# Attention with GpSimd exponentials: wider blocks every third round, the weighing two rounds behind the scores, roots as powers, another first stage and end

## The chip, the core and the metric

The kernel runs on one core of a Trainium2 chip. Its engines have a queue each and meet through semaphores: TensorE (PE in the rows; PEld is its weight load), VectorE (DVE), ScalarE (ACT), GpSimd (POOL) and SyncE (SP), whose queue issues most DMAs. The metric is the device time of one execution, in microseconds; the median of several counts.

## What is computed

One transformer layer with adaptive norms on 4096 tokens of width 256, 16 heads of 16 elements, hidden width 1024.

```python
h = _layernorm(x, axis=-1) * (1 + ca) + sa
x = x + ga * _L0_attn_ref(h, L0_attn_Wq, L0_attn_Wp, L0_attn_bp)
h = _layernorm(x, axis=-1) * (1 + cb) + sb
x = x + gb * _L0_ffn_ref(h, ...)

def _L0_attn_ref(x, Wq, Wp, bp):
    q = jnp.einsum('bnhd,hed->bnhe', xh, Wq)
    scores = jnp.einsum('bnhe,bmhe->bhnm', q, q)
    attn = jax.nn.softmax(scores / NORM, axis=-1)
    res = jnp.einsum('bhnm,bmhe->bnhe', attn, q)
    return res.reshape(B, N, D) @ Wp.T + bp
```

`_L0_ffn_ref` is a norm, two quantised matrix products with a silu between them, and half of the result added to its input. The heavy part is the softmax: 16 x 4096 x 4096 exponentials.

## The kernel before

**First stage** (the first `nc.Block`). The tokens go by in 8 tile groups of 512. For each group VectorE takes the statistics (`stats_of`), the root (`rsqrt`, a bit trick and three Newton steps: 12 small instructions, each waiting for the one ahead), and the normalised tokens (`normalise`, into `z_tok`, two slots). TensorE transposes them (`turn`, L477) and multiplies by `wq_diag`, feature side (L499) and token side (L511). ScalarE rounds to half precision (L440), VectorE keeps the rest (`split`, L582), and SP stores both to DRAM, from where `keys` and `asks` are loaded. VectorE's queue is in an order written by hand: statistics of groups 0 and 1, a root for both, then later groups between the splits.

**Main stage** (the second block). There are 8 x 4 = 32 *groups*: 512 asking tokens (index `c`) times 4 heads. A group has 64 *pairs* of score tiles (a pair is two 128 x 512 tiles, of one head). Three pairs make a *round*, 683 in all; `FIRST[gg]` is the round with which group `gg` begins. In a round:

- TensorE writes the scores of three pairs into six PSUM banks (L894).
- ScalarE takes the exponential of the first two pairs straight from PSUM (L857, 2048 columns).
- VectorE copies the third pair to SBUF (`copy_scores`), which frees its banks early, and ScalarE takes the exponential there (L863, 1024 columns).
- In the rounds of `SPARE_ROUNDS` (292 of the 683) the last `SPARE` = 128 columns of the third pair are GpSimd's: VectorE scales and clamps them (L1092), and GpSimd works out the exponential in eleven instructions of 128 columns (L825 to L841, here called a block); ScalarE then has 896 columns. `has_spare` gives every second round to GpSimd, but none from the 7th to the 20th round of the first group of an asking tile.
- `weigh` multiplies the exponentials with the values (L908), in *units* of four heads, one or two in a round. It waits for `exps_done` and, where a pair has GpSimd columns, for `spare_done`.

TensorE and VectorE run ahead: in the loop turn of round `at` both first serve the scores of round `at + BEHIND` (`scores_of`, `copy_scores`), and then do the weighing and everything else of `at`. `BEHIND` is 1, and `probs` has `P_RING` = 15 places for pairs.

Between these lie the projection, the norms and the feed-forward part of the asking tile before, cut into 40 pieces of TensorE work for each tile (`PIECE_IN`). Their norms are VectorE's, in the first group of the next tile: `norms(o, r)` in round `FIRST + r`. At r = 12 the second half of `x1` is there, and the moments follow (`bn_aggr`, L1121); at 13 and 14 the root; at 15 and 16 the scaling (`modulate`); at 17 and 18 statistics and moments again; at 18 and 19 the second root; at 20 the second norm. GpSimd has nothing to do with these.

**End.** The last asking tile has no attention beside it: sums, projection, norms and feed-forward run in a row, in two `PARTS` of two tiles each.

Of the kernel before, what the change touches and what calls it, by code (L numbers as in the profile page):

```python
# [10 lines left out]
P = 128  # L11
BANK = 512
# [25 lines left out]
S_RING, P_RING, K_RING = 3, 15, 4  # L38
BEHIND = 1
# [3 lines left out]
RSQRT_STEPS = 12  # L43
# [10 lines left out]
PARTS = [(0, 2), (2, 4)]  # L54

# [45 lines left out]
SPARE = 128  # L101
# [8 lines left out]
def has_spare(at):  # L110

    gg = max(g for g in range(GROUPS) if FIRST[g] <= max(at - BEHIND, 0))
    c, group = divmod(gg, Q_GROUPS)
    r = at - BEHIND - FIRST[gg]
    return at % 2 == 0 and at + 1 < ROUNDS and not (c > 0 and group == 0 and 7 <= r <= 20)


SPARE_ROUNDS = [at for at in range(ROUNDS) if has_spare(at)]
# [39 lines left out]


def rsqrt_guess(dve, y, v, work, step, n):  # L160

    shifted, v_eps = work[:, 0, :], work[:, 2, :]
    k = n * RSQRT_STEPS
    dve.tensor_scalar(v_eps, v, EPS, None, ALU.add).then_inc(step, 1)
    dve.wait_ge(step, k + 1)
    dve.tensor_scalar(shifted.bitcast(I32), v_eps.bitcast(I32), 1, None, ALU.logical_shift_right).then_inc(step, 1)
    dve.wait_ge(step, k + 2)
    dve.tensor_scalar(y.bitcast(I32), shifted.bitcast(I32), -1.0, float(0x5F3759DF), ALU.mult, ALU.add).then_inc(step, 1)


def rsqrt_steps(dve, y, work, step, n, steps):

    square, v_eps = work[:, 1, :], work[:, 2, :]
    k = n * RSQRT_STEPS
    for i in steps:
        dve.wait_ge(step, k + (3 + 3 * i))
        dve.tensor_tensor(square, y, y, ALU.mult).then_inc(step, 1)
        dve.wait_ge(step, k + (4 + 3 * i))
        dve.scalar_tensor_tensor(out=square, in0=square, scalar=-0.5, in1=v_eps, op0=ALU.mult, op1=ALU.mult).then_inc(step, 1)
        dve.wait_ge(step, k + (5 + 3 * i))  # L180
        dve.scalar_tensor_tensor(out=y, in0=square, scalar=1.5, in1=y, op0=ALU.add, op1=ALU.mult).then_inc(step, 1)


def rsqrt(dve, y, v, work, step, n):

    rsqrt_guess(dve, y, v, work, step, n)
    rsqrt_steps(dve, y, work, step, n, range(3))
    dve.wait_ge(step, (n + 1) * RSQRT_STEPS)


def adaln_layer(nc, x, wq_t, wp_t, bp, gamma, beta, fc1_q, fc1_s, fc1_b, fc2_q, fc2_s, fc2_b,
# [9 lines left out]
    with ctx:  # L201
# [56 lines left out]
        rsqrt_work = a.take("rsqrt_work", 3 * 5 * GT).rearrange("p (s t) -> p s t", s=3)  # L258
# [26 lines left out]
        stats_done, moments_done, rstd_done, z_ready = sem("stats_done"), sem("moments_done"), sem("rstd_done"), sem("z_ready")  # L285
# [73 lines left out]
        with nc.Block() as block:  # L359

            @block.sync
            def _(sp):
# [41 lines left out]

                sp.wait_ge(shift_split, 1)
                first_shifts(sp, 0)
                stored(G - 1)
                load_keys(sp, 3, 1)
                stored(G - 2)

            @block.gpsimd
            def _(pool):
                pool.memset(ones, 1.0).then_inc(c_step, 1)
                pool.memset(values[:, :, :, E:E1], 1.0).then_inc(ones_set, 1)
                pool.wait_ge(ones_set, 1)
# [46 lines left out]
            def _(pe):  # L462
                pe.wait_ge(c_step, 4)
# [6 lines left out]
                pe.wait_ge(const_in, 16)  # L470

                def turn(g):
                    pe.wait_ge(z_ready, g + 1)
# [21 lines left out]
                for g in range(G):  # L495
# [5 lines left out]
                    if g == 2:  # L501
                        keep_running(pe, ps_turn[:, 0, 0:P], ident[:, :], 22)
# [53 lines left out]
            def _(dve):  # L556
# [10 lines left out]
                def rstd_of(first, last, n):  # L567
                    dve.wait_ge(moments_done, last)
                    rsqrt(dve, rstd[:, first * GT:last * GT], moments[:, first * GT:last * GT, 1],
                          rsqrt_work[:, :, 0:(last - first) * GT], rstd_done, n)  # L570
# [795 lines left out]
```

## Time and profile before

| | us |
|---|---|
| median of 3 runs (2000.42 to 2002.87) | 2001.24 |
| the profiled execution | 2002.06 |
| its span, first to last instruction | 2000.0 |
| ScalarE busy | 1907.8 |
| TensorE busy (matmul ends are modelled) | 1884.5 |
| GpSimd busy | 1269.7 |
| VectorE busy | 1239.2 |

The first stage ends, and the first exponential begins, at 80.94; the last exponential of the main stage begins at 1941.51 and the end takes the rest. In the rows below, a timeline row gives start and duration in us, engine, line and operation, output<-input with sizes, how many instructions it merges (x), and in brackets the idle time ahead with what ended it.

### The profile page before, as it was taken

To read this page: it belongs to the slowest core of one execution; us is meant where nothing else is said; L and a number is where in the kernel's file an instruction comes from. 1 tells how busy PE (TensorE), PEld (TensorE's weight loads), DVE (VectorE), ACT (ScalarE), POOL (GpSimd) and SP (SyncE) were. 2 spreads that over 40 slices of the span, in tenths; PEclk is the share of its full clock that TensorE was granted. 3 is DMA by queue.
4 is the path that set the end of the run, shared out by engine and by line. 5 is a ranking of instruction groups with operands and counts; after the bars stand their busy time and mean duration, and the time that the engine had idled before them with its cause. 6 is when DMAs were issued, how large, how long until landed. Compare 5 with 4: busy or idle time off the path is not lost.

```text
span 2000.0 us, 47347 instructions
## 1 busy us (share of the span) xinstructions
PE 1884.5 (94%) x18477; PEld 549.5 (27%) x18477; DVE 1239.2 (62%) x1925; ACT 1907.8 (95%) x1491; POOL 1269.7 (63%) x3218
## 2 busy tenths in 40 slices
PE   6888889999999999999999999999999999999998
PEld 4411112222222222222222222222222222222235
DVE  7456555766576655766557665765657665576645
ACT  3799999999999999999999999999999999999982
POOL 0288775478836787177854788367872788547860
PEclk9899999999999999999999999999999999999999
DMA  5441111121211212112211212112121112111100
GB/s 166 136 148 38 46 52 43 46 55 47 53 42 50 56 44 62 45 43 49 58 48 48 57 43 54 41 53 53 45 61 48 41 49 58 48 39 45 32 12 13
DMA packets 121376, 108.40 MB, mean 54 GB/s; under 512 B 21936, under 2 KB 120112, under 8 KB 120896
## 3 DMA queue, kind: packets, MB, share of 16 engines
q1 hardware_dynamic: 120400, 103.69, 19.5%
q8 instruction: 147, 2.41, 0.5%
q10 hardware_dynamic: 752, 1.67, 0.2%
q14 instruction: 77, 0.63, 0.1%
HBM read 96.49 MB, written 8.65 MB: 53 GB/s over the span
## 4 chain that ended last, share of the span: by engine, by line
ACT 69%; PE 16%; issue 9%; DVE 2%; ACTq 0%; DVEq 0%
ACT attend_probs L857 40%; ACT attend_probs L863 29%; PE attend_sums L908 7%; PE attend_scores L894 4%; PE attend_out L916 3%; PE attend_scores L916 1%; ACT attend_half_tanh L851 1%; DVE attend_probs L1096 0%; PE attend_out L922 0%; PE attend_sums L922 0%; DVE w L1255 0%; DVE attend_st L1114 0%; DVE attend_x L1081 0%; ACT attend_att_feat L869 0%; PE attend_scores L922 0%
## 5 line engine op out<-in xcount | busy, mean ns | idle before, releaser
L857 ACT ACTIVATE attend_probs<-attend_scores 128x2048 f32<-128x2048 f32 x683 | 1294.8, 1896 | 7.8 <-PE attend_scores L894 4.7
L908 PE MATMUL attend_sums<-attend_probs,values 128*17 128x512 f32 x8192 | 1006.9, 597 | 1.2 <-POOL attend_probs L841 1.2
L1096 DVE COPY attend_probs<-attend_scores 128x1024 f32<-128x1024 f32 x390 | 477.4, 1224 | 372.4 <-PE attend_scores L894 367.7
L863 ACT ACTIVATE attend_probs<-attend_probs 128x1024 f32<-128x1024 f32 (+1 forms) x682 | 702.2, 1030 | 1.9 <-DVE attend_probs L1096 1.9
L894 PE MATMUL attend_scores<-asks,keys 64*128 64x512 f16 x4096 | 562.7, 380 | 85.9 <-ACT attend_probs L857 72.1
L825 POOL TENSOR_SCALAR attend_spare<-attend_probs 128x128 f32<-128x128 f32 x292 | 90.6, 310 | 473.9 <-DVE attend_probs L1092 466.3
L894 PEld LDWEIGHTS attend_scores<-asks,keys 64*128 64x128 f16 x4096 | 149.4, 94 | 686.7 <-ACT attend_probs L857 566.1
L1094 DVE COPY attend_probs<-attend_scores 128x896 f32<-128x896 f32 x292 | 315.5, 1081 | 0.0
L908 PEld LDWEIGHTS attend_sums<-attend_probs,values 128*17 128x17 f32 x8192 | 174.1, 96 | 510.9 <-issue 483.1
L1092 DVE TENSOR_SCALAR attend_probs<-attend_scores,gains 128x128 f32<-128x128 f32 x292 | 102.4, 351 | 266.2 <-PE attend_scores L894 263.9
L829 POOL TENSOR_TENSOR attend_spare<-attend_probs,attend_spare 128x128 f32<-128x128 f32 x292 | 147.9, 506 | 24.3
L839 POOL TENSOR_TENSOR attend_spare<-attend_spare 128x128 f32<-128x128 f32 x292 | 147.4, 505 | 22.9
L841 POOL TENSOR_TENSOR attend_probs<-attend_spare 128x128 f32<-128x128 f32 x292 | 141.4, 484 | 22.9
L836 POOL TENSOR_TENSOR attend_spare<-attend_spare,attend_probs 128x128 f32<-128x128 f32 x292 | 139.0, 476 | 24.3
L837 POOL TENSOR_TENSOR attend_spare<-attend_spare,attend_probs 128x128 f32<-128x128 f32 x292 | 137.6, 471 | 0.0
L831 POOL TENSOR_TENSOR attend_probs<-attend_spare 128x128 f32<-128x128 f32 x292 | 117.5, 403 | 22.9
L916 PE MATMUL attend_out<-w,hidden 128*32 128x256 f32 x1920 | 124.2, 379 | 0.0
L916 PE MATMUL attend_out<-attend_att_feat,w 128*32 128x512 f32 x896 | 116.6, 592 | 0.0
L827 POOL TENSOR_SCALAR attend_spare<-attend_spare 128x128 f32<-128x128 f32 x292 | 89.3, 306 | 24.1
L834 POOL TENSOR_SCALAR attend_spare<-attend_spare 128x128 int32<-128x128 f32 x292 | 92.4, 316 | 18.2
L832 POOL TENSOR_SCALAR attend_spare<-attend_spare 128x128 f32<-128x128 f32 x292 | 89.4, 306 | 19.7
L833 POOL TENSOR_SCALAR attend_spare<-attend_spare 128x128 f32<-128x128 f32 x292 | 88.7, 304 | 18.2
(160 smaller groups left out, 907.5 us busy)
## 6 DMA issues: line engine op xcount, KB each, us to landing
keys<-parts_dram SPq DMA_DIRECT2D x768, 64.0 KB
keys<-parts_dram SPq DMA_DIRECT2D x256, 56.0 KB
asks<-parts_dram SPq DMA_DIRECT2D x192, 64.0 KB
start_x_in<-L_attn_x SPq DMA_DIRECT2D x8, 512.0 KB, 9.5
parts_dram<-start_q_parts SPq DMA_DIRECT2D x16, 256.0 KB, 2.5
attend_x_now<-L_attn_x SPq DMA_DIRECT2D x8, 512.0 KB, 4.4
out<-base SPq DMA_DIRECT2D x16, 256.0 KB, 2.6
asks<-parts_dram SPq DMA_DIRECT2D x64, 56.0 KB
```

Of the source, the lines that this page charges most:

```text
L829: pool.tensor_tensor(part, cols, whole, ALU.subtract).then_inc(spare_step, 1)
L836: pool.tensor_tensor(first, first, cols, ALU.add)
L837: pool.tensor_tensor(second, second, cols, ALU.add).then_inc(spare_step, 1)
L839: pool.tensor_tensor(first, first, second, ALU.mult).then_inc(spare_step, 1)
L841: pool.tensor_tensor(cols, first, whole, ALU.mult).then_inc(spare_done, 1)
L857: act.activation(place(n, 2), ps_scores[:, 0:4, :], ACT.Exp, scale=scale).then_inc(exps_done, 1)
L863: act.activation(cols, cols, ACT.Exp, scale=scale).then_inc(exps_done, 1)
L894: last = pe.matmul(ps_scores[:, 2 * i + b, :], keys[rows, part % K_RING, hq, col:col + P], asks[rows, group * Q_HEADS + hq, :], start=True ...
L908: last = pe.matmul(ps_sums[32 * hq:32 * hq + E1, :], values[:, j + STEPS * b, (gg % Q_GROUPS) * Q_HEADS + hq, :], place(gg * PAIRS + Q_HEA ...
L916: last = pe.matmul(to[32 * q:32 * q + 32, :], held[:, 32 * q:32 * q + 32], moved, start=start, stop=stop)
L1094: dve.tensor_copy(flat(n, 0, DIRECT), bank[:, 0:DIRECT]).then_inc(copied, 1)
L1096: dve.tensor_copy(flat(n, 0, 2 * BANK), bank).then_inc(copied, 1)
```

## The change

- `SPARE` is 256 columns instead of 128, and a block goes to 213 rounds instead of 292: a round at least three after the last one, and only if the pair is weighed in the loop turn of `at + 2` or later. The rounds of the norms are no longer left out.
- `BEHIND` is 2 and `P_RING` 18, so weighing, pieces and norms follow the scores by one more round. The room comes from smaller DMA scratch and from tanh being written straight into `hidden`.
- Every root becomes a power on GpSimd: add EPS, then `pow` with -0.5 (`power`). In the main stage `MOMENTS_IN` puts it into GpSimd's queue behind the block of the rounds `FIRST + 12` and `FIRST + 18`. VectorE has `centre` at r = 13 and 14 instead of the root.
- First stage: GpSimd takes the powers and, for groups 1 to 7, the normalised tokens; VectorE normalises group 0 alone, behind the statistics of that group only. TensorE has 14 filler matmuls ahead of the first columns and 14 behind them.
- End: sums, division, transposes and the powers by halves, the second part's transposes ahead of the first part's last products, one more and smaller last store.

The core of the diff:

```diff
-S_RING, P_RING, K_RING = 3, 15, 4
-BEHIND = 1
+S_RING, P_RING, K_RING = 3, 18, 4
+BEHIND = 2
-SPARE = 128
+SPARE = 256
-    return at % 2 == 0 and at + 1 < ROUNDS and not (c > 0 and group == 0 and 7 <= r <= 20)
+        if weighed_in(S_RING * at + 2) >= at + 2 and (not rounds or at - rounds[-1] >= 3):
+            rounds.append(at)
+MOMENTS_IN = {FIRST[Q_GROUPS * c] + r: (2 * (c - 1) + i, i) for c in range(1, G) for i, r in enumerate((12, 18))}
...
+                    pool.wait_ge(moments_done, g + 1)
+                    pool.tensor_scalar(v_eps[:, tiles], moments[:, tiles, 1], 1.0, EPS, ALU.mult, ALU.add).then_inc(eps_added, 1)
+                    pool.wait_ge(eps_added, g + 1)
+                    pool.tensor_tensor(rstd[:, tiles], v_eps[:, tiles], minus_half, ALU.pow).then_inc(rstd_done, 1)
...
+                        last = pool.tensor_scalar(z_tok[:, g % 2, t, :], x_in[:, tile, :],
+                                                  minus_mean[:, tile:tile + 1], rstd[:, tile:tile + 1], ALU.add, ALU.mult)
...
+                keep_running(pe, ps_qf[:, 0, 0:P], ident[:, :], 14)
...
+                def power(n, r, tiles):
+                    pool.wait_ge(n_mom, n + 1)
+                    pool.tensor_scalar(v_eps[:, r, tiles], mo2[:, r, tiles, 1], 1.0, EPS, ALU.mult, ALU.add).then_inc(eps2_added, 1)
+                    pool.wait_ge(eps2_added, n + 1)
+                    pool.tensor_tensor(rs2[:, r, tiles], v_eps[:, r, tiles], minus_half[:, tiles], ALU.pow).then_inc(n_rstd, 1)
...
+                for at in range(ROUNDS):
+                    if at in SPARE_ROUNDS:
+                        exps(k, at)
+                        k += 1
+                    if at in MOMENTS_IN:
+                        power(*MOMENTS_IN[at], slice(0, GT))
```

GpSimd's queue at the first moments of the first asking tile (round 98). Before, blocks follow each other, the last of round 92 and the next of round 108:

```order
L837 TENSOR_TENSOR attend_spare<-attend_spare,attend_probs 128x128
L839 TENSOR_TENSOR attend_spare<-attend_spare 128x128 [waits spare_step]
L841 TENSOR_TENSOR attend_probs<-attend_spare 128x128 [waits spare_step]
L825 TENSOR_SCALAR attend_spare<-attend_probs 128x128 [waits spare_in,spare_done]
L827 TENSOR_SCALAR attend_spare<-attend_spare 128x128 [waits spare_step]
```

Now the block of round 96, the power, and the block of round 99 (`attend_mo` holds the moments, `attend_rs` the roots):

```order
L832 TENSOR_TENSOR attend_spare<-attend_spare 128x256 [waits spare_step]
L834 TENSOR_TENSOR attend_probs<-attend_spare 128x256 [waits spare_step]
L810 TENSOR_SCALAR attend_v_eps<-attend_mo 128x4 [waits n_mom]
L812 TENSOR_TENSOR attend_rs<-attend_v_eps,attend_minus_half 128x4 [waits eps2_added]
L818 TENSOR_SCALAR attend_spare<-attend_probs 128x256 [waits spare_in,spare_done]
```

Two instructions with a wait for VectorE's moments have moved in between two blocks.

VectorE's queue at the same place, before:

```order
L1081 TENSOR_TENSOR attend_x<-attend_out,attend_x_now 128x512 [waits proj_mm]
L1114 BN_STATS attend_st<-attend_x 128x6 [waits x1_ready]
L1114 BN_STATS attend_st<-attend_x 128x6
L1121 BN_AGGR attend_mo<-attend_st 128x2 [waits n_stats]
L1121 BN_AGGR attend_mo<-attend_st 128x2 x3
L1096 COPY attend_probs<-attend_scores 128x1024 [waits steps_done,scores_ready]
L164 TENSOR_SCALAR attend_rsqrt_work<-attend_mo 128x4 [waits n_mom]
```

and now:

```order
L1110 TENSOR_SCALAR attend_probs<-attend_scores,gains 128x256 [waits steps_done,scores_ready]
L1112 COPY attend_probs<-attend_scores 128x768
L1114 COPY attend_probs<-attend_scores 128x1024 [waits steps_done,scores_ready]
L1099 TENSOR_TENSOR attend_x<-attend_out,attend_x_now 128x512 [waits proj_mm]
L1132 BN_STATS attend_st<-attend_x 128x6 [waits x1_ready]
L1132 BN_STATS attend_st<-attend_x 128x6
L1139 BN_AGGR attend_mo<-attend_st 128x2 [waits n_stats]
L1139 BN_AGGR attend_mo<-attend_st 128x2 x3
L1114 COPY attend_probs<-attend_scores 128x1024 [waits steps_done,scores_ready]
L1147 SCALAR_TENSOR_TENSOR attend_hid<-attend_x,attend_mo,mod 128x256 [waits n_mom]
```

The moments stand behind the copy of round 100 instead of 99: L1110 and L1112 are round 99 with its 256 columns for GpSimd, and L1114 is round 100. Behind them stands `centre` (L1147) where the root was.

## Rows read from the trace of the kernel before

**Rows 1.** Page: busy time, share of the span and instructions of each engine.

```profile
PE 1884.5 (94%) x18477; PEld 549.5 (27%) x18477; DVE 1239.2 (62%) x1925; ACT 1907.8 (95%) x1491; POOL 1269.7 (63%) x3218
```

**Rows 2.** Groups by line and shape: busy us, mean ns | idle before, what ended it.

```profile
L857 ACT ACTIVATE attend_probs<-attend_scores 128x2048 f32<-128x2048 f32 x683 | 1294.8, 1896 | 7.8 <-PE attend_scores L894 4.7
L908 PE MATMUL attend_sums<-attend_probs,values 128*17 128x512 f32 x8192 | 1006.9, 597 | 1.2 <-POOL attend_probs L841 1.2
...
L863 ACT ACTIVATE attend_probs<-attend_probs 128x1024 f32<-128x1024 f32 x390 | 419.2, 1075 | 1.9 <-DVE attend_probs L1096 1.9
...
L863 ACT ACTIVATE attend_probs<-attend_probs 128x896 f32<-128x896 f32 x292 | 283.0, 969 | 0.0
...
L1136 DVE SCALAR_TENSOR_TENSOR attend_hid<-attend_x,attend_mo,mod 128x256 f32<-128x256 f32 x28 | 12.2, 477 | 0.0
```

**Rows 3.** Timeline: ScalarE in a plain round and a GpSimd round, TensorE's scores.

```profile
999.11 1.91 ACT L857 ACTIVATE attend_probs<-attend_scores 128x2048 f32<-128x2048 f32 x1
...
1001.83 1.90 ACT L857 ACTIVATE attend_probs<-attend_scores 128x2048 f32<-128x2048 f32 x1
...
1003.78 0.82 PE L894 MATMUL attend_scores<-asks,keys 64*128 64x512 f16 x6
...
1004.43 1.90 ACT L857 ACTIVATE attend_probs<-attend_scores 128x2048 f32<-128x2048 f32 x1
...
1004.53 1.91 PE L908 MATMUL attend_sums<-attend_probs,values 128*17 128x512 f32 x16
```

**Rows 4.** Timeline: first and last instruction of one GpSimd block, that of round 1001.83.

```profile
1002.45 0.30 POOL L825 TENSOR_SCALAR attend_spare<-attend_probs 128x128 f32<-128x128 f32 x1 [0.40 <-DVE attend_probs L1092]
...
1006.83 0.46 POOL L841 TENSOR_TENSOR attend_probs<-attend_spare 128x128 f32<-128x128 f32 x1
```

**Rows 5.** Timeline: GpSimd at two widths, the only such pair.

```profile
0.25 0.10 POOL L1360 MEMSET const-float32-0.0<- 128x1 f32 x1 [0.25 <-issue]
...
0.74 0.20 POOL L413 MEMSET start_ones<- 128x128 f32 x1 [0.29 <-POOLq L1360]
```

**Rows 6.** Timeline: VectorE's moments, each with the round then on ScalarE (100, 105, 184).

```profile
351.08 1.89 ACT L857 ACTIVATE attend_probs<-attend_scores 128x2048 f32<-128x2048 f32 x1
351.84 0.38 DVE L1121 BATCH_NORM_AGGREGATE attend_mo<-attend_st 128x2 f32<-128x6 f32 x4
...
365.15 1.89 ACT L857 ACTIVATE attend_probs<-attend_scores 128x2048 f32<-128x2048 f32 x1
366.38 0.37 DVE L1121 BATCH_NORM_AGGREGATE attend_mo<-attend_st 128x2 f32<-128x6 f32 x4
...
580.75 1.93 ACT L857 ACTIVATE attend_probs<-attend_scores 128x2048 f32<-128x2048 f32 x1
582.80 0.38 DVE L1121 BATCH_NORM_AGGREGATE attend_mo<-attend_st 128x2 f32<-128x6 f32 x4
```

**Rows 7.** Timeline: GpSimd's last instruction of a block beside VectorE's L1189.

```profile
399.25 0.77 DVE L1189 SCALAR_TENSOR_TENSOR hidden<-attend_half_tanh,attend_half_in 128x512 f32<-128x512 f32 x1
399.55 0.79 POOL L841 TENSOR_TENSOR attend_probs<-attend_spare 128x128 f32<-128x128 f32 x1
```

**Rows 8.** Timeline: the first stage, L499 of groups 0, 6 and 7, and the first split.

```profile
16.18 1.94 PE L477 MATMUL start_ps<-ident,start_z_tok 128*128 128x128 f32 x8 [5.99 <-DVE start_z_tok L576]
...
19.81 1.96 PE L499 MATMUL start_ps<-start_h_feat,start_wq_diag 128*128 128x512 f32 x4 [0.72 <-ACT start_h_feat L429]
...
26.72 1.28 DVE L582 SCALAR_TENSOR_TENSOR start_q_parts<-start_ps,gains,start_q_parts 128x1024 f16<-128x1024 f32 x1
...
60.47 1.88 PE L499 MATMUL start_ps<-start_h_feat,start_wq_diag 128*128 128x512 f32 x4
...
65.58 1.88 PE L499 MATMUL start_ps<-start_h_feat,start_wq_diag 128*128 128x512 f32 x4
```

**Rows 9.** Timeline: the end, one root on VectorE, and the second part's transposes.

```profile
1955.49 0.17 DVE L164 TENSOR_SCALAR attend_rsqrt_work<-attend_mo 128x2 f32<-128x2 f32 x1
...
1957.86 0.74 DVE L1307 TENSOR_SCALAR z<-attend_x,attend_mo,attend_rs 128x256 f32<-128x256 f32 x2
...
1980.38 1.06 PE L916 MATMUL attend_scores<-ident,z 128*32 128x128 f32 x32
```

More of the change, by code:

```diff
@@ L107, with weighed_in, spare_rounds @@
 LEAD_BITS = float((127 - 7) * 2 ** 23 + 1887232)
[L110 to L114, printed above, removed]
-    return at % 2 == 0 and at + 1 < ROUNDS and not (c > 0 and group == 0 and 7 <= r <= 20)
-SPARE_ROUNDS = [at for at in range(ROUNDS) if has_spare(at)]
+def weighed_in(n):
+    gg, p = divmod(n, PAIRS)
+    for r, (begin, end) in enumerate(units(gg)):
+        if begin <= 2 * (p // Q_HEADS) < end:
+            return FIRST[gg] + r
+    return FIRST[gg + 1]
+def spare_rounds():
+    rounds = []
+    for at in range(BEHIND, ROUNDS - 1):
+        if weighed_in(S_RING * at + 2) >= at + 2 and (not rounds or at - rounds[-1] >= 3):
+            rounds.append(at)
+    return rounds
+SPARE_ROUNDS = spare_rounds()
+MOMENTS_IN = {FIRST[Q_GROUPS * c] + r: (2 * (c - 1) + i, i) for c in range(1, G) for i, r in enumerate((12, 18))}
 def spares_to(n):
@@ L626, in _ @@
                 last.then_inc(bound_step, 1)
[L628 to L634 removed]
+                stats_of(1)
                 dve.wait_ge(bound_mm, 1)
@@ L917, in by_columns, with turn @@
                     return last
-                def turn(bank, source):
-                    for t in range(GT):
+                def turn(bank, source, tiles=range(GT)):
+                    for t in tiles:
                         for q in range(4):
@@ L1122, in bn_aggr, with centre @@
                     last.then_inc(n_mom, 1)
-                def root(r, n, part):
-                    if part == 0:
-                        dve.wait_ge(n_mom, n + 1)
-                        rsqrt_guess(dve, rs2[:, r, :], mo2[:, r, :, 1], rsqrt_work2, n_rstd, n)
-                    rsqrt_steps(dve, rs2[:, r, :], rsqrt_work2, n_rstd, n, [(0,), (1, 2)][part])
-                def modulate(o, half):
-                    tiles = range(2 * half, 2 * half + 2)
-                    dve.wait_ge(n_rstd, (2 * o + 1) * RSQRT_STEPS)
+                def centre(o, half):
                     wait(dve, base_step, 3 * o)
-                    for t in tiles:
+                    dve.wait_ge(n_mom, 2 * o + 1)
+                    for t in range(2 * half, 2 * half + 2):
                         last = dve.scalar_tensor_tensor(out=hid[:, t, :], in0=x1[:, t, :], scalar=mo2[:, 0, t, 0:1], in1=mod[:, 2, :],
@@ L1138, in modulate @@
                     last.then_inc(scaled, 1)
+                def modulate(o, half):
+                    dve.wait_ge(n_rstd, 2 * o + 1)
                     dve.wait_ge(scaled, 2 * o + half + 1)
-                    for t in tiles:
+                    for t in range(2 * half, 2 * half + 2):
                         last = dve.scalar_tensor_tensor(out=hid[:, t, :], in0=hid[:, t, :], scalar=rs2[:, 0, t:t + 1], in1=mod[:, 1, :],
@@ L1162, in norms @@
                     elif r in (13, 14):
-                        root(0, 2 * o, r - 13)
+                        centre(o, r - 13)
                     elif r in (15, 16):
```

258 lines of the change are left out of this document (133 added, 125 removed).

## The prediction

> **What bounds the kernel now.** I read the busy shares first [rows 1]: ScalarE 95%, TensorE 94%, the others some 63%. Busy TensorE is modelled, so the groups with their idle time decide [rows 2]: between all 683 rounds ScalarE waits 7.8 us ahead of L857 and 1.9 ahead of L863. The main stage is ScalarE's, end to end. In the timeline [rows 3] a plain round takes 1001.83 - 999.11 = 2.72 us and a GpSimd round 1004.43 - 1001.83 = 2.60. TensorE has little room all the same: the scores of the next round start at 1003.78, 0.05 after L857 has ended, last 0.82 and free the weighing at 1004.53, and ScalarE wants the scores at 1004.43. Work that TensorE does late by more than about 0.45 us (0.25 of its own waiting, 0.2 between the first two pairs and ScalarE's next start; an estimate from these rows) delays ScalarE. GpSimd never does this now: L908 waits 1.2 us for L841 in the whole run [rows 2]. The first stage (81 us) and the end (57 us) are chains, bound by their waits.
>
> **ScalarE's columns.** L863 takes 1075 ns for 1024 columns and 969 for 896 [rows 2]: 106 ns for 128. Now 292 x 0.106 = 31.0 us are saved; after, 213 x 0.212 = 45.2. Gain **14.2 us**.
>
> **GpSimd's block at 256 columns.** A block lasts from 1002.45 to 1006.83 + 0.46, so 4.84 us [rows 4], and no instruction of this kind at 256 columns is in the trace. The nearest rows are two fills [rows 5]: 0.10 us for 1 column, 0.20 for 128, so at least 0.10 more for each of eleven instructions: 4.84 + 1.1 = 5.95. At the other end only 0.10 of each is fixed and the rest doubles: the five short ones (0.30) gain 0.20 each, the six others (0.46) some 0.36, so 4.84 + 1.0 + 2.1 = 7.95. Nothing says which; I take the middle, **7.0**. Three rounds of ScalarE, one of them with GpSimd, last 2 x 2.72 + 2.49 = 7.93, and the 213 blocks are 3.2 rounds apart on average, so a block of 7.0 keeps pace.
>
> **The powers in GpSimd's queue.** This is where the change gives back. GpSimd is in order, and in round 98 its queue now has a wait for VectorE's moments, ahead of the block of round 99. Before, these moments end at 351.84 + 0.38 = 1.14 us after the start of round 100 on ScalarE [rows 6]. VectorE and TensorE now serve the scores of one more round first, so they end 1.14 after the start of round 101. Round 99 is a GpSimd round (2.49), round 100 plain: 2.49 + 2.72 + 1.14 = 6.35 us after the start of round 99. The power itself is two instructions of 4 columns; with rows from 0.10 to 0.46 [rows 3 to 5] and 0.08 between (1002.45 to 1006.83 has such gaps) it is 0.36 to 1.1, and since a power is no plain operation, the far bound is the whole root on VectorE, 1957.86 - 1955.49 = 2.37 [rows 9]. I take 0.95. The block begins at 7.3 and ends at 14.3, where it would have ended at some 7.8. TensorE weighs that pair in loop turn 101, behind the scores of round 103, which start when round 102 has done its L857: 2.49 + 2 x 2.72 + 1.9 + 0.75 = 10.6. It waits 3.7, and ScalarE loses 3.2.
>
> The 14 moments fall into three patterns, since a tile is 85 1/3 rounds. Rounds 98, 354 and 610: 3.2 each. Rounds 183 and 439: moments at 2.43 after a start [rows 6], so 2.49 + 2.43 + 0.95 + 7.0 = 12.9 against 10.6: 1.85. The second moments of these five tiles (104, 360, 616; 189 and 445 alike): 1.60 after a start [rows 6], so 2.49 + 1.60 + 0.95 + 7.0 = 12.05: 1.0. Rounds 268, 274, 524 and 530: the next block is two to four rounds off, nothing. Sum: 3 x 3.2 + 2 x 1.85 + 5 x 1.0 = 18.3. Behind each, GpSimd makes up the delay at 7.93 - 7.0 = 0.9 a block, so further blocks are late, but inside their room.
>
> These are also the rounds in which VectorE works with two operands in SBUF, eight of `centre` and `modulate` at 0.48 us [rows 2], just behind the moments. Beside such an instruction GpSimd stands: L841 takes 0.79 instead of 0.46 while L1189 runs until 400.02 [rows 7]. So GpSimd loses about 0.2 us for each of the eight, 1.6 in a first moment's block, 5 x 1.6 = 8. Before, no block lay there. The Trainium skill's page "SBUF — State Buffer" (§ Who interferes with whom) states this for a VectorE instruction with two SBUF inputs against a GpSimd instruction that reads SBUF: who comes first holds the port for its whole instruction, the other blocks fully. [rows 7] agree for GpSimd's side, and no row shows VectorE's. By the rule VectorE would be held up as well, by up to one GpSimd instruction, now up to 0.8 us wide, for each of the eight; if its copies of the third pairs came late by a fourth of these 6.4 us in five tiles, ScalarE would lose 8 more and the sum below would be 2004. By the rows it loses nothing, since a late VectorE has 38% idle time [rows 1] to make it up, and I stay with them.
>
> Together the moments cost **26 us**. With a block of 5.95 it is 26 - 10 x 1.05 = 15, with 7.95 it is 36; without the losses beside VectorE 8 less. The main stage then comes out 26 - 14.2 = **12 us longer**. `BEHIND` = 2 costs nothing elsewhere (18 places for pairs hide it), and VectorE's short root instructions in this stage were off the path.
>
> **First stage.** L499 of groups 6 and 7 are 5.11 apart [rows 8], TensorE's own pace. From group 0 to 7 it is 65.58 - 19.81 = 45.77, where 7 x 5.11 = 35.8 would do: 10.0 are lost because the first split waits until 26.72 behind statistics and roots, and the like later. With roots and tokens on GpSimd, VectorE has only splits and statistics. GpSimd then needs, for each group, two small instructions, a power and four of 256 columns: between 5 x 0.1 + 4 x 0.3 = 1.7 and 2.4 + 0.4 + 4 x 0.9 = 6.4 us; under 5.11 for most of that, so I count the whole 10. Group 0 starts earlier by one group's statistics and half a root, but 28 filler matmuls now stand ahead of it, which makes -4 to +3; I take +1.5. Gain **11.5 us** (4 to 14).
>
> **End.** Of the four roots (2.37 each, [rows 9]) the two of the first part are on the path; a power with two hand-overs takes 1.2, and `centre` covers some of the first: 2.9 saved. The second part's transposes (1.06 at 1980.38) and ScalarE's work behind them leave the path: 1.5. Halves and the small store: 1. Gain **5.5 us** (1 to 7).
>
> **The sum.** 2002.06 + 12 - 11.5 - 5.5 = 1997 for the profiled execution, which was 0.8 above the median of the runs: **1996 us**.
>
> **Rivals.**
> - *The waits do not bite.* A block near 5.95 and a quick power: moments 9, so -5 in the main stage, -14 and -7 outside: **1976**. For it: the fills. Against it: a sum of two tensors is not a fill.
> - *The powers cost more.* On the other side, slower: the one wait for moments, with a power of 2 us or a block near 7.9. The moments then cost 40 to 50, the first stage gains 8, the end 2: about **2017**. It decides from a power of about 1.5 us, or a block of 7.6. For it: the power has no row, and lateness piles up once a block nears 7.93.
> - *GpSimd becomes the bound.* From a block of 8.5 us (3.2 rounds) on. If every instruction doubled outright (9.2), 213 x 9.3 = 1981 against a main stage of 1848: **2100**. For it: nothing but the missing row.
>
> **How the numbers follow.** The forecast has 0.50, spread over 1986 to 2006 by its own bounds; the quiet waits 0.18, the dear powers 0.25, GpSimd as the bound 0.07. About 0.2% (4 us) is what a measurement of this kernel tells from no change. Faster by more: 0.27 of the forecast and all of the quiet case, 0.45. Slower by more: 0.06 of the forecast, 0.22 of the dear powers, GpSimd as the bound, 0.35. Within: the rest, 0.20. The range leaves out GpSimd as the bound, the far end of the dear powers and half of the quiet case's lower half: 1977 to 2027.
>
> **What would show it.** In the trace after: L863 at 768 columns near 0.86 us; the block between its first and last instruction (7.0); GpSimd idle for some 5 us ahead of the power in round 98, and L913 (the weighing) waiting 3 to 5 us for `spare_done` five rounds later, in five of seven tiles; elsewhere rounds of 2.72 and 2.49; the first exponential near 69.5; 51 us from the last exponential to the end. If the weighing waits all over the stage, GpSimd is the bound; if it waits nowhere, my placing of the moments is wrong.

## The result, and the profile after

The changed kernel takes 2027.97 us (median of 4 runs, 2027.43 to 2030.63) against 2001.37 for the kernel before on the same chip: a ratio of 1.0135, 95% interval 1.0122 to 1.0148. It is 1.35% slower; the forecast was 1996, its range 1977 to 2027. The profiled execution has a span of 2025.4 us.

The page's row of busy time answers to [rows 1]:

```profile
PE 1894.1 (94%) x18453; PEld 548.3 (27%) x18453; DVE 1208.2 (60%) x1572; ACT 1911.7 (94%) x1491; POOL 1433.0 (71%) x2438
```

ScalarE has as much to do as before (1911.7 against 1907.8), although GpSimd now works 163 us more. The groups by line and shape answer to [rows 2]; columns are busy us, mean ns, then idle time just before and what ended it. L862, L868 and L913 are what L857, L863 and L908 were before, L834 is the last instruction of a block, L810 the first of a power, L812 the power itself; L1156 belongs to `modulate`, L1164 is the second norm:

```profile
L862 ACT ACTIVATE attend_probs<-attend_scores 128x2048 f32<-128x2048 f32 x683 | 1281.7, 1877 | 41.3 <-PE attend_scores L899 40.1
L913 PE MATMUL attend_sums<-attend_probs,values 128*17 128x512 f32 x8192 | 1015.0, 601 | 29.1 <-POOL attend_probs L834 29.0
...
L868 ACT ACTIVATE attend_probs<-attend_probs 128x1024 f32<-128x1024 f32 x469 | 493.9, 1053 | 6.8 <-DVE attend_probs L1114 6.8
...
L868 ACT ACTIVATE attend_probs<-attend_probs 128x768 f32<-128x768 f32 x213 | 181.2, 851 | 2.3 <-DVE attend_probs L1112 2.3
...
L1156 DVE SCALAR_TENSOR_TENSOR attend_hid<-attend_hid,attend_rs,mod 128x256 f32<-128x256 f32 x28 | 19.4, 732 | 0.0
...
L1164 DVE TENSOR_SCALAR z<-attend_hid,attend_mo,attend_rs 128x256 f32<-128x256 f32 x28 | 19.2, 744 | 0.0
...
L812 POOL TENSOR_TENSOR attend_rs<-attend_v_eps,attend_minus_half 128x4 f32<-128x4 f32 x14 | 14.3, 1024 | 1.2
...
L810 POOL TENSOR_SCALAR attend_v_eps<-attend_mo 128x4 f32<-128x4 f32 x14 | 2.8, 199 | 58.9 <-DVE attend_mo L1139 58.7
```

Three numbers are new. ScalarE waits 41.3 us for scores (7.8 before), TensorE's weighing waits 29.0 us for late blocks (1.2 before), and GpSimd waits 58.7 us ahead of the powers for VectorE's moments. GpSimd's wait is no loss in itself; what is queued behind it is.

ScalarE's first and last exponential of two pairs, in the timeline (start, duration, in us); the first two rows are those of the kernel before, the other two of the changed kernel:

```profile
80.94 1.88 ACT L857 ACTIVATE attend_probs<-attend_scores 128x2048 f32<-128x2048 f32 x1 [1.79 <-PE attend_scores L894]
...
1941.51 1.89 ACT L857 ACTIVATE attend_probs<-attend_scores 128x2048 f32<-128x2048 f32 x1
```

```profile
69.22 1.88 ACT L862 ACTIVATE attend_probs<-attend_scores 128x2048 f32<-128x2048 f32 x1 [3.76 <-PE attend_scores L899]
...
1972.67 1.88 ACT L862 ACTIVATE attend_probs<-attend_scores 128x2048 f32<-128x2048 f32 x1
```

So the first stage is 11.7 us shorter, the main stage lasts 1903.45 in place of 1860.57, which is 42.9 longer, and the end takes 52.7 in place of 58.5, which is 5.8 shorter. The whole loss lies in the main stage, and two stretches of the timeline show its two kinds.

**An ordinary GpSimd round**, as in [rows 3], with the block's first and last instruction:

```profile
1002.72 1.89 ACT L862 ACTIVATE attend_probs<-attend_scores 128x2048 f32<-128x2048 f32 x1
...
1003.55 0.41 POOL L818 TENSOR_SCALAR attend_spare<-attend_probs 128x256 f32<-128x256 f32 x1 [3.00 <-DVE attend_probs L1110]
...
1004.48 0.86 ACT L868 ACTIVATE attend_probs<-attend_probs 128x768 f32<-128x768 f32 x1
...
1004.67 0.82 PE L899 MATMUL attend_scores<-asks,keys 64*128 64x512 f16 x6
1005.31 1.88 ACT L862 ACTIVATE attend_probs<-attend_scores 128x2048 f32<-128x2048 f32 x1
...
1009.77 0.73 POOL L834 TENSOR_TENSOR attend_probs<-attend_spare 128x256 f32<-128x256 f32 x1
```

The block lasts 1009.77 + 0.73 - 1003.55 = 6.95 us. The round lasts 1005.31 - 1002.72 = 2.59, no less than with 128 columns (2.60). It is made of L862's 1.89, 0.06 until the next scores start, since they go into the banks that L862 reads, and 0.64 until their first two pairs have arrived. L868 is not in this chain.

**A moment.** Round 98 and those behind it, all engines:

```profile
344.85 0.20 POOL L810 TENSOR_SCALAR attend_v_eps<-attend_mo 128x4 f32<-128x4 f32 x1 [7.23 <-DVE attend_mo L1139]
...
346.14 0.41 POOL L818 TENSOR_SCALAR attend_spare<-attend_probs 128x256 f32<-128x256 f32 x1
...
349.42 1.88 ACT L862 ACTIVATE attend_probs<-attend_scores 128x2048 f32<-128x2048 f32 x1
...
352.79 0.72 POOL L834 TENSOR_TENSOR attend_probs<-attend_spare 128x256 f32<-128x256 f32 x1
...
353.66 3.19 PE L913 MATMUL attend_sums<-attend_probs,values 128*17 128x512 f32 x16 [4.06 <-POOL attend_probs L834]
...
357.43 1.88 ACT L862 ACTIVATE attend_probs<-attend_scores 128x2048 f32<-128x2048 f32 x1 [5.18 <-PE attend_scores L899]
```

GpSimd idles 7.23 us, the block of round 99 starts at 346.14 and ends at 353.51, TensorE waits 4.06 for it, and round 103 of ScalarE lasts 357.43 - 349.42 = 8.01 us in place of 2.72: 5.3 lost for a wait of 4.06. The rest is the weighing, 16 matmuls in 3.19 us where 1.91 is usual. The table by windows shows why (length, busy time of each engine, then the granted clock, DMA share, GB/s):

```profile
354.00:357.00 3.00, 3.00 (x18) 0.51 (x12) 0.00 (x0) 0.00 (x0) 2.57 (x6) 0.62 0.00 0
357.00:360.00 3.00, 2.22 (x20) 0.44 (x16) 2.35 (x3) 2.57 (x2) 2.75 (x5) 1.00 0.01 3
```

After the wait TensorE has a granted clock of 0.62, part of the time on the lower of its two levels (1.2 of 2.4 GHz), until it is back at 1.00.

Such stalls come at the places that the prediction named: in rounds 13 to 27 of the seven tiles with norms the kernel loses, against before, 8.9, 5.6, 0.6, 9.3, 4.1, 0.6 and 8.9 us. The two small ones are the tiles of rounds 268 and 524, where the next block is farther off.

### The profile page after: what moved, and what is told of

The parts are those of the page before. It is cut to its first block, busy times and chain, and to the rows that moved or that the text cites. A ratio compares the mean times of both kernels' runs of the same rounds, so it can differ in the third digit from the quotient of the medians.

```text
span 2025.4 us, 45992 instructions
## 1 busy us (share of the span) xinstructions
PE 1894.1 (94%) x18453; PEld 548.3 (27%) x18453; DVE 1208.2 (60%) x1572; ACT 1911.7 (94%) x1491; POOL 1433.0 (71%) x2438
## 4 chain that ended last, share of the span: by engine, by line
ACT 58%; PE 26%; issue 9%; POOL 4%; DVE 3%; SPq 0%; DMA 0%; POOLq 0%; DVEq 0%
ACT attend_probs L862 34%; ACT attend_probs L868 22%; PE attend_sums L913 11%; PE attend_scores L899 7%; PE attend_out L921 4%; PE attend_scores L921 1%; ACT hidden L856 1%; PE attend_sums L927 1%; PE start_ps L513 1%; DVE attend_probs L1114 1%; PE start_ps L503 1%; POOL attend_rs L812 1%; PE attend_out L927 0%; DVE attend_sums_sb L1076 0%; POOL attend_spare L830 0%
## 5 line engine op out<-in xcount | busy, mean ns | idle before, releaser
L862 ACT ACTIVATE attend_probs<-attend_scores 128x2048 f32<-128x2048 f32 x683 | 1281.7, 1877 | 41.3 <-PE attend_scores L899 40.1
L913 PE MATMUL attend_sums<-attend_probs,values 128*17 128x512 f32 x8192 | 1015.0, 601 | 29.1 <-POOL attend_probs L834 29.0
L1114 DVE COPY attend_probs<-attend_scores 128x1024 f32<-128x1024 f32 x469 | 574.0, 1224 | 465.1 <-PE attend_scores L899 460.2
L868 ACT ACTIVATE attend_probs<-attend_probs 128x1024 f32<-128x1024 f32 (+1 forms) x682 | 675.1, 990 | 9.2 <-DVE attend_probs L1114 6.8
L913 PEld LDWEIGHTS attend_sums<-attend_probs,values 128*17 128x17 f32 x8192 | 175.6, 96 | 541.9 <-issue 423.1
L818 POOL TENSOR_SCALAR attend_spare<-attend_probs 128x256 f32<-128x256 f32 x213 | 87.8, 412 | 305.1 <-DVE attend_probs L1110 303.0
L1110 DVE TENSOR_SCALAR attend_probs<-attend_scores,gains 128x256 f32<-128x256 f32 x213 | 102.9, 483 | 219.3 <-PE attend_scores L899 216.5
L1112 DVE COPY attend_probs<-attend_scores 128x768 f32<-128x768 f32 x213 | 201.8, 947 | 0.0
L822 POOL TENSOR_TENSOR attend_spare<-attend_probs,attend_spare 128x256 f32<-128x256 f32 x213 | 169.1, 794 | 17.7
L832 POOL TENSOR_TENSOR attend_spare<-attend_spare 128x256 f32<-128x256 f32 x213 | 165.1, 775 | 16.7
L834 POOL TENSOR_TENSOR attend_probs<-attend_spare 128x256 f32<-128x256 f32 x213 | 160.4, 753 | 16.7
L829 POOL TENSOR_TENSOR attend_spare<-attend_spare,attend_probs 128x256 f32<-128x256 f32 x213 | 157.3, 738 | 17.7
L830 POOL TENSOR_TENSOR attend_spare<-attend_spare,attend_probs 128x256 f32<-128x256 f32 x213 | 161.5, 758 | 0.0
L824 POOL TENSOR_TENSOR attend_probs<-attend_spare 128x256 f32<-128x256 f32 x213 | 131.9, 619 | 16.7
L827 POOL TENSOR_SCALAR attend_spare<-attend_spare 128x256 int32<-128x256 f32 x213 | 94.4, 443 | 13.3
L825 POOL TENSOR_SCALAR attend_spare<-attend_spare 128x256 f32<-128x256 f32 x213 | 91.3, 428 | 14.4
L820 POOL TENSOR_SCALAR attend_spare<-attend_spare 128x256 f32<-128x256 f32 x213 | 86.9, 408 | 17.6
L826 POOL TENSOR_SCALAR attend_spare<-attend_spare 128x256 f32<-128x256 f32 x213 | 87.5, 411 | 13.3
```

The source lines that it names most:

```text
L822: pool.tensor_tensor(part, cols, whole, ALU.subtract).then_inc(spare_step, 1)
L829: pool.tensor_tensor(first, first, cols, ALU.add)
L830: pool.tensor_tensor(second, second, cols, ALU.add).then_inc(spare_step, 1)
L832: pool.tensor_tensor(first, first, second, ALU.mult).then_inc(spare_step, 1)
L834: pool.tensor_tensor(cols, first, whole, ALU.mult).then_inc(spare_done, 1)
L862: act.activation(place(n, 2), ps_scores[:, 0:4, :], ACT.Exp, scale=scale).then_inc(exps_done, 1)
```

## The experiments

Two theories had to be told apart from others. **Queue:** a power waits in GpSimd's queue ahead of a block, and TensorE then waits for that block. **Floor:** from 896 columns on, the chain of L862 and the next scores ends a GpSimd round, so that taking more columns off ScalarE saves nothing. The kernel before took 2001.37 us beside the changed kernel and 2001.66 and 2002.07 beside the two sets of experiments, so medians of different sets can be compared to within about 1 us.

**Everything but the first stage and the end undone.**

```
-S_RING, P_RING, K_RING = 3, 18, 4
-BEHIND = 2
+S_RING, P_RING, K_RING = 3, 15, 4
+BEHIND = 1
...
-SPARE = 256
+SPARE = 128
...
-SPARE_ROUNDS = spare_rounds()
+SPARE_ROUNDS = [at for at in range(ROUNDS) if has_spare(at)]
...
-                    if at in MOMENTS_IN:
-                        power(*MOMENTS_IN[at], slice(0, GT))
...
+                        root(0, 2 * o, r - 13)
```

> The changed kernel with its main stage put back: blocks of 128 columns every second round with the old exclusion, one round behind, 15 places, and the roots of the main stage on VectorE again. What is left of the change is the first stage and the end. Theory: the traces show 11.7 us less to the first exponential and 5.8 less behind the last, and nothing ties them to the main stage, so 2001 - 17.5 = 1984 us, with a main stage of 1861 between first and last exponential. Rival (part of the main stage's loss comes in from the new first stage, such as its later loads or a clock that is lower at its start): 1988 or more, and a main stage of 1865 or more.

Measured: 1982.77 us (1981.48 to 1985.42), ratio to before 0.9912 (0.9895 to 0.9928); main stage 1859.11. The two outer parts are worth 18.9 us, and none of the main stage's loss comes in from the first stage.

```profile
69.04 1.88 ACT L886 ACTIVATE attend_probs<-attend_scores 128x2048 f32<-128x2048 f32 x1 [3.75 <-PE attend_scores L923]
...
1927.92 3.63 PE L937 MATMUL attend_sums<-attend_probs,values 128*17 128x512 f32 x32
1928.15 1.89 ACT L886 ACTIVATE attend_probs<-attend_scores 128x2048 f32<-128x2048 f32 x1
```

The end is shorter here than in the changed kernel, 50.85 us behind the last exponential in place of 52.68. TensorE's weighing row of 32 matmuls starts 0.23 before the last exponential; in the changed kernel, which works two rounds behind, the same row starts 1.62 after it (1972.67):

```profile
1974.29 3.62 PE L913 MATMUL attend_sums<-attend_probs,values 128*17 128x512 f32 x32
```

All the other kernels with `BEHIND` = 2 end as the changed one does, in 52.6 to 52.7 us. So that part of the change costs 1.8 us at the end.

**The roots of the main stage back on VectorE.**

```
-                    if at in MOMENTS_IN:
-                        power(*MOMENTS_IN[at], slice(0, GT))
...
+                        root(0, 2 * o, r - 13)
...
+                        root(1, 2 * o + 1, 0)
```

> The changed kernel with one part undone: the roots of the main stage are VectorE's short instructions again, in the old loop turns, and GpSimd's queue in that stage holds blocks alone. Theory (the power's wait for VectorE's moments holds the block behind it, TensorE waits for that block and its clock falls): the losses in rounds 97 to 110 and their like, 37.9 us in seven tiles, go; VectorE's short instructions are hidden. 1990 us, at most 1996 if blocks beside centre and modulate still run late. Rival (the losses come from the norms' work one round later and from VectorE and GpSimd holding each other up, not from the queue): most of the 38 us stays, 2015 or more.

Measured: 2013.89 us (2013.54 to 2015.58), ratio 1.0065 (1.0048 to 1.0082). That is 24 us more than the theory said and just under the rival's 2015. TensorE's waits for blocks are gone, and yet every one of the seven tiles loses 3.4 to 3.6 us in rounds 13 to 27, also those that lost only 0.6 before. The groups say who is late now (L893 and L1139 are this kernel's L868 and L1114; L193 is the last step of a root):

```profile
L938 PE MATMUL attend_sums<-attend_probs,values 128*17 128x512 f32 x8192 | 1006.6, 597 | 0.0
...
L893 ACT ACTIVATE attend_probs<-attend_probs 128x1024 f32<-128x1024 f32 x469 | 494.1, 1053 | 24.6 <-DVE attend_probs L1139 24.3
...
L193 DVE SCALAR_TENSOR_TENSOR attend_rs<-attend_rsqrt_work,attend_rs 128x4 f32<-128x4 f32 x42 | 12.8, 304 | 1.4
```

VectorE's timeline in the root behind the second moment, and what follows on ScalarE:

```profile
362.40 0.58 DVE L180 TENSOR_SCALAR attend_rs<-attend_rsqrt_work 128x4 int32<-128x4 int32 x1
363.02 0.65 DVE L189 TENSOR_TENSOR attend_rsqrt_work<-attend_rs 128x4 f32<-128x4 f32 x1
363.70 0.16 DVE L191 SCALAR_TENSOR_TENSOR attend_rsqrt_work<-attend_rsqrt_work 128x4 f32<-128x4 f32 x1
363.90 0.58 DVE L193 SCALAR_TENSOR_TENSOR attend_rs<-attend_rsqrt_work,attend_rs 128x4 f32<-128x4 f32 x1
364.41 1.21 DVE L1139 COPY attend_probs<-attend_scores 128x1024 f32<-128x1024 f32 x1
...
365.65 1.06 ACT L893 ACTIVATE attend_probs<-attend_probs 128x1024 f32<-128x1024 f32 x1 [1.26 <-DVE attend_probs L1139]
```

Instructions of 4 columns, 0.16 us when undisturbed (L191), take 0.58 to 0.65 while GpSimd's block runs beside them with instructions of up to 0.73. The copy of the third pair is then late, and ScalarE waits 1.26 us.

**The blocks left out beside VectorE's roots.** The kernel above with one thing more undone:

```
     for at in range(BEHIND, ROUNDS - 1):
+        gg = max(g for g in range(GROUPS) if FIRST[g] <= at - BEHIND)
+        if gg > 0 and gg % Q_GROUPS == 0 and 7 <= at - BEHIND - FIRST[gg] <= 20:
+            continue
```

> The kernel with VectorE's roots (2013.9) with one thing more undone: no blocks in loop turns 7 to 20 of a tile with norms, as before the change; 184 blocks in place of 213. Theory (its loss of 3.4 us in each of seven tiles is VectorE and GpSimd holding each other up: root instructions of 0.16 us take up to 0.65, modulate 0.85 in place of 0.48, and VectorE's copies come late): 24 us less, 29 x 0.135 = 4 more for the blocks left out, 1994. Rival (the loss comes from the norms' work standing one round later in TensorE's and VectorE's turns): no less than 2013, 2018 with the blocks left out.

Measured: 1991.83 us (1991.18 to 1994.06), ratio 0.9953 (0.9937 to 0.9970). That is 22.1 us less; the first theory said 20, the rival none.

```profile
L896 ACT ACTIVATE attend_probs<-attend_probs 128x1024 f32<-128x1024 f32 x498 | 527.4, 1059 | 2.3 <-DVE attend_probs L1142 2.1
...
L196 DVE SCALAR_TENSOR_TENSOR attend_rs<-attend_rsqrt_work,attend_rs 128x4 f32<-128x4 f32 x42 | 6.8, 162 | 1.5
```

The same root step takes 162 ns where no block lies beside it, in place of 304. `BEHIND` = 2, which this kernel still has, loses nothing there (0.1 us a tile in rounds 13 to 27, against the kernel before).

**The powers one loop turn later.**

```
-MOMENTS_IN = {... for i, r in enumerate((12, 18))}
+MOMENTS_IN = {... for i, r in enumerate((13, 19))}
```

> The changed kernel with one number changed: each power stands one loop turn later in GpSimd's queue, so behind the next block in place of ahead of it. Theory: GpSimd no longer idles for the moments with a block queued behind the wait, TensorE's waits for L834 (29 us) go nearly all, and the time is 1990 to 1996; VectorE now waits up to 1 us for the second power ahead of z2, which may cost up to 0.8 us in five tiles. Rival (the losses come from the norms' later work, whatever the queue's order): 2015 or more. Second rival (the power's own 1.3 us makes the following block late all the same): about 2005.

Measured: 1991.87 us (1990.56 to 1993.12), ratio 0.9951 (0.9934 to 0.9967). Only two entries of a table differ (13 and 19 for 12 and 18), no work is added or taken away, and it is 36.1 us less than the changed kernel.

```profile
L913 PE MATMUL attend_sums<-attend_probs,values 128*17 128x512 f32 x8192 | 1006.9, 597 | 0.0
```

```profile
69.79 1.88 ACT L862 ACTIVATE attend_probs<-attend_scores 128x2048 f32<-128x2048 f32 x1 [4.34 <-PE attend_scores L899]
...
1938.53 1.88 ACT L862 ACTIVATE attend_probs<-attend_scores 128x2048 f32<-128x2048 f32 x1
```

The weighing waits for no block any more, and the queue theory stands; the main stage lasts 1868.74 us. The power itself is no burden: in the groups of this run, VectorE's instructions that use the roots have no idle time ahead of them. In rounds 13 to 27 a tile now loses 0.1 to 0.6 us against the kernel before.

**Fillers ahead of TensorE's waits**, to price the clock alone:

```
+                            if c in (1, 2, 4, 5, 7) and gg % Q_GROUPS == 0 and r in (15, 21):
+                                pe.wait_ge(x1_ready, 2 * c)
+                                keep_running(pe, ps_out[:, 0:P], ident[:, :], 13 if r == 15 else 8)
                             pe.wait_ge(spare_done, spares_to(last_pair))
```

> The changed kernel with matmuls without use put into TensorE's stream ahead of its waits for the late blocks: 13 in loop turn 15 (some 3.0 us, from 44 matmuls in 5.18 at the end) and 8 in turn 21 (1.9 us) of the five tiles whose weighing waits; the waits themselves stay. Theory (behind the wait the granted clock is 0.56 to 0.62, which makes the weighing take 3.19 in place of 1.91 us and the like: 1.28 + 0.96 in three tiles, 1.64 in two, 10.0 in all, on the path): 2028 - 10 = 2018. Rival (the slow stretch is covered by other work, or the fillers last longer than the waits): 2028 or more.

Measured: 2020.73 us (2019.12 to 2022.41), ratio 1.0098 (1.0081 to 1.0115): 7.2 less than the changed kernel, where 10.0 was expected. The edit did half of what was said: the second weighing of a tile stands in the first turn of the next group, which the condition does not reach, so only the 13 fillers of the first waits are in the program (130 matmul records in five tiles, two for each filler). For these the expected sum is 3 x 1.28 + 2 x 1.64 = 7.1, but that it is so near the 7.2 is partly luck, as the rounds below show. The first wait of the first tile, the round behind it, and its second wait:

```profile
350.62 3.17 PE L168 MATMUL attend_out<-ident 128*128 128x128 f32 x26
354.66 1.91 PE L917 MATMUL attend_sums<-attend_probs,values 128*17 128x512 f32 x16 [0.87 <-POOL attend_probs L834]
...
357.15 1.88 ACT L862 ACTIVATE attend_probs<-attend_scores 128x2048 f32<-128x2048 f32 x1 [3.81 <-PE attend_scores L899]
...
372.70 1.91 PE L917 MATMUL attend_sums<-attend_probs,values 128*17 128x512 f32 x16 [2.07 <-POOL attend_probs L834]
```

```profile
354.00:357.00 3.00, 2.34 (x22) 0.58 (x22) 0.00 (x0) 0.00 (x0) 2.67 (x5) 1.00 0.01 3
```

The granted clock is 1.00 behind the wait, the weighing takes 1.91 us again, though the block ends as late as before, and ScalarE waits 3.81 us in place of 5.18. The same holds for the first waits of all five tiles; their rounds are 6.3 us shorter in all than in the changed kernel's profiled execution. The second waits have no fillers ahead of them. Yet in three tiles the clock stayed at 1.00 behind them this time (4.7 us less), and in one, where it had been 1.00, it was 0.64 (1320 to 1324; 1.6 us more). So the fillers show what the lower clock costs behind the first waits, some 6 us; behind the second ones it came and went without them.

**Fewer columns for ScalarE**, to test the floor from below:

```
-  cols = flat(n + 2, 0, DIRECT if at in SPARE_ROUNDS else 2 * BANK)
+  cols = flat(n + 2, 0, DIRECT - 256 if at in SPARE_ROUNDS else 2 * BANK)
```

> The changed kernel in which ScalarE does 512 columns of the third pair in a GpSimd round, in place of 768; the exponentials of the other 256 columns are left out. Everything else stands. Theory (a GpSimd round of 2.58 us is not ScalarE's any more: the next scores go into the banks that L862 reads, so a round is at least L862's 1.88, a hand-over, two pairs of scores and a hand-over): rounds stay at 2.58, time 2028 within 2. Rival (my prediction's step: a column of ScalarE is worth its own time, 106 ns for 128): 0.21 x 213 = 45 us less, 1983, with rounds of 2.37.

Measured: 2027.35 us (2027.05 to 2027.69), ratio 1.0130 (1.0113 to 1.0147): no gain over the 2027.97 of the changed kernel.

```profile
L862 ACT ACTIVATE attend_probs<-attend_scores 128x2048 f32<-128x2048 f32 x683 | 1281.1, 1876 | 82.1 <-PE attend_scores L899 81.4
...
L868 ACT ACTIVATE attend_probs<-attend_probs 128x512 f32<-128x512 f32 x213 | 135.6, 637 | 2.3 <-DVE attend_probs L1112 2.3
```

L868 is 851 - 637 = 214 ns shorter, 45.6 us in all, and L862 waits 82.1 - 41.3 = 40.8 us longer for scores. ScalarE's freed time turned into idle time nearly one for one.

**Narrow blocks in the same rounds**, the floor from above: the kernel with the later powers and

```
-SPARE = 256
+SPARE = 128
```

> The kernel with the later powers (1991.9) with one size changed: blocks of 128 columns in the same 213 rounds, so ScalarE does 896 columns there in place of 768. Theory (from 896 columns on the next scores end the round): GpSimd rounds 2.60 in place of 2.58, 213 x 0.02 = 4 us more, 1996; a little less where blocks of 256 still run late behind the powers. Rival (each 128 columns are worth 106 ns): 213 x 0.106 = 23 us more, 2014.

Measured: 1991.57 us (1991.40 to 1992.56), ratio 0.9951 (0.9934 to 0.9968), the same as with 256 columns.

```profile
L868 ACT ACTIVATE attend_probs<-attend_probs 128x1024 f32<-128x1024 f32 x469 | 503.1, 1073 | 2.4 <-DVE attend_probs L1114 2.4
...
L868 ACT ACTIVATE attend_probs<-attend_probs 128x896 f32<-128x896 f32 x213 | 207.8, 976 | 0.0
```

The second half of GpSimd's columns is worth nothing. From the start of one L862 to the next, the median GpSimd round lasts 2.58 us with 512 columns for ScalarE (the run above), 2.58 with 768 (the changed kernel) and 2.60 to 2.61 with 896 (the kernel before and this run); a plain round lasts 2.71 to 2.72. The main stage lasts 1867.52 us, still 7.0 more than before with the same narrow blocks: it has 213 GpSimd rounds, not 292. The 4 us that the rounds of 2.60 should have cost are paid back by VectorE: ScalarE waits 2.4 us for its copies in place of 7.3 (5.0 and 2.3 by the groups of the kernel with 256 columns).

**Narrow blocks every second round, everywhere**, which might have beaten all others (`power_round` gives the round behind whose block a power now stands):

```
-SPARE = 256
+SPARE = 128
...
-        if ... and (not rounds or at - rounds[-1] >= 3):
+        if ... and (not rounds or at - rounds[-1] >= 2):
...
+def power_round(at):
+    return at + 2 if at + 2 in SPARE_ROUNDS else at + 1
```

> The changed kernel with blocks of 128 columns in every second round of the whole main stage (340 blocks, none left out beside the norms) and each power behind the block that is under way when its moments end. Theory: a GpSimd round saves 0.12 us over a plain one whether 128 or 256 columns are taken, so 340 x 0.12 = 41 us against 292 x 0.12 = 35 in the kernel with the new first stage and end alone (1982.8); with 0.4 us for each tile's moments, as in the run with the later powers, 1982.8 - 5.8 + 2.8 = 1980 us. Rival (GpSimd busy in 4.84 of each 5.3 us beside VectorE's norms makes VectorE's copies late, as with VectorE's roots): 1.5 to 3.4 us for each of seven tiles, 1988 to 2001.

Measured: 1982.51 us (1981.44 to 1984.12), ratio 0.9905 (0.9889 to 0.9922). This is the fastest time here, but no different from the 1982.77 of the kernel that has the two outer parts alone: main stage 1858.83 against 1859.11.

```profile
L873 ACT ACTIVATE attend_probs<-attend_probs 128x1024 f32<-128x1024 f32 x342 | 365.3, 1068 | 4.9 <-DVE attend_probs L1119 4.9
L873 ACT ACTIVATE attend_probs<-attend_probs 128x896 f32<-128x896 f32 x340 | 328.9, 967 | 0.3 <-DVE attend_probs L1117 0.3
```

Of the 5.8 us that 48 more blocks should save, 3.3 go into ScalarE's waits for VectorE (5.2 here; the kernel of the outer parts has 1.9). Where the remaining 2.2 went was not settled.

## Why the prediction was wrong, point by point

| step | forecast | measured | from |
|---|---|---|---|
| ScalarE's columns | -14.2 | +8.2 | main stage with the later powers, 1868.74, against 1860.57 |
| moments in GpSimd's queue | +26 | +34.7 | 1903.45 - 1868.74 (36.1 by the medians) |
| first stage | -11.5 | -11.7 | first exponential |
| end | -5.5 | -5.8 | last exponential to the end of the span |

The errors of the first two are 22.4 and 8.7, 31.1 of the 32 us between 1996 and the result. The +8.2 is all that the new main stage loses once the powers stand behind the blocks, so VectorE's late copies are in it too.

**The step that failed is "Gain 14.2 us".** It priced a column by ScalarE's own time, 106 ns for 128, in a round that ScalarE no longer ends. [rows 3] had it all: the GpSimd round before is 2.60 = 1.90 (L857) + 0.05 (until the scores start) + 0.65 (until the next L857), a chain through the score banks without L863. With 896 columns the two chains end about together, so a shorter L863 leaves the other one in charge. The prediction read the same rows as room, "0.2 between the first two pairs and ScalarE's next start", and took it for slack of TensorE instead of asking what a shorter L863 would leave in charge. So it forecast rounds of 2.49; they are 2.58. The old kernel saves 292 x 0.12 = 35 us over plain rounds, the new 213 x 0.135 = 29, so fewer and wider blocks lose 6. That the floor is there is shown from both sides, by 512 columns (no gain) and by 896 (no loss). VectorE's late copies beside the wider blocks come on top: ScalarE waits 7.3 us for them, 2.4 with narrow blocks and 1.9 before. These 6 and 5 do not add up to the 8.2 exactly; how much of them overlaps was not settled.

**The moments: mechanism and places right, the waits too small and one cost left out.** In round 98 the wait was sized well, 3.7 us forecast and 4.06 measured. Over all ten the prediction's own steps give 3 x 3.7 + 2 x 2.3 + 5 x 1.45 = 23.0, and 29.0 were measured. The pieces in round 98: moments 6.35 after the start of round 99 (6.56 measured), power and hand-overs 0.95 (1.38, of it 1.02 for the power), block 7.0 (7.37 here, 6.95 as a rule). The step "It waits 3.7, and ScalarE loses 3.2" took room off the wait, and the traces show next to none: with the fillers, at a granted clock of 1.00, round 103 lasts 6.64 us in place of 2.72, so 3.9 are lost. In the changed kernel 5.3 are lost, more than the wait, since TensorE's clock falls in it. With the fillers 2020.73 - 1991.87 = 28.9 us of the 36.1 remain, about the 29.0 of the waits. The 8 us that the forecast added for GpSimd's loss beside `centre` and `modulate` were too much: the block of round 99 is 0.42 us longer than others, not 1.6, and the like in the other four tiles.

**VectorE is held up as well.** "By the rows it loses nothing", the prediction said. It does lose: L1156 takes 732 ns where such an instruction took 477 [rows 2], and the second norm's L1164 takes 744 where it took 407 before:

```profile
L1149 DVE TENSOR_SCALAR z<-attend_hid,attend_mo,attend_rs 128x256 f32<-128x256 f32 x28 | 9.6, 407 | 0.0
```

ScalarE's waits for VectorE's copies rise from 1.9 to 9.1 us. This is the half of a rule that the prediction set aside: the Trainium skill's page "SBUF — State Buffer" (§ Who interferes with whom) has the one of the two engines that comes second stand still, whichever it is. The traces agree for both sides. The 8 us more that the prediction gave for it are near the 7.2 of these waits, but by luck, since it put them behind `centre` and `modulate` in five tiles: 5.3 of the 7.2 stand in one round of each of the seven tiles, behind the second norm, whose instructions have a single tensor as input. The same section lets an instruction with a single input take the shared ports in some modes, and L1164 and L180 (0.58 us in place of 0.17) agree with that. With the roots on VectorE it is 22 us, the difference between blocks and no blocks beside them. So the claim that VectorE's short root instructions "were off the path" holds for the kernel before only, where no block lay beside them.

**What held.** The block at 256 columns, 7.0 forecast and 6.95 measured (the median; the mean is 7.17), between the two bounds that the fills gave; L868 at 768 columns, 0.86 and 0.851; the first stage, since GpSimd's part of a group, about 4 us, fits into the period of 5.11. `BEHIND` = 2 costs nothing in the rounds of the norms, 0.1 us a tile. The end came out as forecast, 5.5 and 5.8, but by two things that cancel: with `BEHIND` = 1 the same edits save 7.6, and `BEHIND` = 2, which the prediction called free, takes 1.8 of that back.

**The rivals.** The time came out nearest to "the powers cost more", 2017, but that mechanism did not happen: the power is 1.02 us, not 1.5 or more, and the block is not 7.6. The case that did happen, a round with a floor, was not among them. The main stage of 1848 in the last rival follows from no row (1860.6 less 14.2 is 1846), but nothing else rests on it.

## What to carry to other kernels

Before a column is taken off the busiest engine, look which chain ends the round in which it lies: add up the other path around the loop (here the read of a bank, the hand-over, the next write into it) and count a gain only down to that. A wait that is put into an in-order queue costs what stands behind it; move the wait behind the block that could already run, and the same work costs almost nothing (36 us here for two entries of a table). And a wait of TensorE can be dearer than its length, since the work behind it may run at the lower clock (5.3 us lost for 4.06 here, 3.9 where fillers kept the clock up).

## What the runs showed of the hardware

- A power on GpSimd takes 1.02 us for 128x4 elements, while a multiply and add of the same shape takes 0.20.
- GpSimd's instructions from 128 to 256 columns: one tensor and two constants 0.30 to 0.41 us, two tensors 0.46 to 0.73. If the time grows evenly with the columns, some 0.19 us of each is fixed (an estimate from these two sizes), which lies between the two bounds taken.
- VectorE instructions of 4 columns stretch from 0.16 to as much as 0.65 us beside GpSimd, also with a single tensor as input (L180, 0.58 us). Those of 256 columns with a single tensor as input go from 407 to 744 ns on average (L1149, L1164).
- A wait of TensorE of 2.07 us was followed by a granted clock of 0.56 in one tile (373 to 376 us) and of 1.00 in another (612 to 615), as these two rows of the changed kernel's table by windows show. With fillers ahead of the first wait of the first tile, its second wait, again 2.07 us, was followed by 1.00. What tells these apart was not tried.

```profile
373.00:376.00 3.00, 3.00 (x16) 0.55 (x16) 0.31 (x1) 1.06 (x1) 2.63 (x6) 0.56 0.03 5
612.00:615.00 3.00, 2.25 (x20) 0.63 (x22) 1.36 (x2) 1.44 (x2) 2.67 (x5) 1.00 0.00 0
```
